# The score of each expert spread by a DMA from DRAM instead of a selection matmul, in a fused macaron block of two MoE layers on one core

## The reference, cut to what matters

```python
def _L0_ffn_ref(hidden_states, router_w, router_b, gate_up_proj, gate_up_bias, down_proj, down_bias):
    B, S, H, E, K, I = (1, 64, 128, 16, 4, 128)
    ALPHA, LIMIT = (1.702, 7.0)
    x = hidden_states.reshape(-1, h)
    logits = x @ router_w + router_b
    topv, topi = jax.lax.top_k(logits, K)
    topw = jax.nn.softmax(topv, axis=-1)
    one_hot = (topi[..., None] == jnp.arange(E)).astype(topw.dtype)
    scores = jnp.einsum('tk,tke->te', topw, one_hot)
    gu = jnp.einsum('th,ehf->tef', x, gate_up_proj) + gate_up_bias
    gate = jnp.minimum(gu[..., ::2], LIMIT)
    up = jnp.clip(gu[..., 1::2], -LIMIT, LIMIT)
    glu = gate * jax.nn.sigmoid(gate * ALPHA)
    act = (up + 1.0) * glu
    expert_out = jnp.einsum('tei,eih->teh', act, down_proj) + down_bias
    out = jnp.einsum('te,teh->th', scores, expert_out)

x = x + 0.5 * _L0_ffn_ref(_layernorm(x), ...)      # first FFN
x = x + _L0_attn_ref(_layernorm(x), ...)           # state-space mixer, with an inner layer norm
x = x + 0.5 * _L0_ffn_ref(_layernorm(x), ...)      # the same FFN and weights again
```

## Time and profile before

| | |
|---|---|
| Time, median of 3 runs | 824.15 us (819.81 to 825.55) |
| The profiled execution: time, span | 822.77 us, 821.0 us |
| Engine busy in it | PE 718.6, DVE 497.7, ACT 568.1, POOL 261.4 us |
| Jobs, first selection matmul to last | 28.3 to 394.4 us |
| The passes two to eight (jobs 16 to 127) | 80.7 to 396.6 us |

### The profile page before, as it was taken

One profiled execution on the slowest core, in us unless ns is written; L12 is line 12 of the kernel. 1 busy time (PEld: TensorE's weight loads), 2 busy tenths in 40 slices (PEclk: granted clock), 3 DMA queues, 4 the chain that ended last, 5 costly groups with the idle time before them and its releaser, 6 DMA issues.

```text
span 821.0 us, 11243 instructions
## 1 busy us (share of the span) xinstructions
PE 718.6 (88%) x3736; PEld 429.3 (52%) x3736; DVE 497.7 (61%) x1268; ACT 568.1 (69%) x800; POOL 261.4 (32%) x289
## 2 busy tenths in 40 slices
PE   2889889899898999999686696999999999999587
PEld 2567667676676777878564352323323232233364
DVE  4789878789788888888566442244423232222464
ACT  4557675667777666555344446999999999999243
POOL 2286466665666554555412000021200000000020
PEclk9999999999999999999758776999999999999958
DMA  9100000000000000000000269100079400000001
GB/s 269 42 0 2 0 1 1 0 1 2 0 1 1 0 1 2 0 1 1 0 1 0 52 127 196 36 1 1 1 134 194 85 2 1 1 1 1 3 1 51
DMA packets 14989, 24.94 MB, mean 30 GB/s; under 512 B 2720, under 2 KB 11376, under 8 KB 13424
## 3 DMA queue, kind: packets, MB, share of 16 engines
q1 hardware_dynamic: 13776, 23.79, 13.2%
q0 software_dynamic: 224, 0.34, 0.2%
q10 hardware_dynamic: 928, 0.06, 0.1%
HBM read 6.35 MB, written 1.05 MB: 9 GB/s over the span
## 4 chain that ended last, share of the span: by engine, by line
ACT 28%; PE 14%; issue 9%; DVE 5%; POOL 4%; ACTq 0%; POOLq 0%; DVEq 0%
ACT raw_w L782 25%; POOL act_parts L539 3%; PE bank L1341 2%; PE bank L1342 2%; PE bank L1343 2%; PE bank L1628 1%; ACT xt L609 1%; PE bank L1381 1%; PE bank L1535 1%; PE bank L1396 1%; PE bank L1612 1%; DVE xn_parts L875 1%; PE bank L1397 1%; POOL rstd L488 1%; DVE stats L865 1%
## 5 line engine op out<-in xcount | busy, mean ns | idle before, releaser
L782 ACT ACTIVATE raw_w<-bank,minus_c 128x1024 f32<-128x1024 f32 x256 | 259.3, 1161 | 4.8 <-DVE bank L1221 2.6
L539 POOL TENSOR_TENSOR act_parts<-act,act_parts 128x512 fp32r<-128x512 f32 x128 | 168.5, 1318 | 151.1 <-ACT act_parts L671 148.2
L657 ACT ACTIVATE glu<-bank,b_gate 128x512 f32<-128x512 f32 x128 | 88.1, 688 | 113.5 <-PE bank L1343 112.8
L1221 DVE TENSOR_TENSOR bank<-bank,fix 128x256 f32<-128x256 f32 x128 | 55.3, 433 | 180.4 <-PE bank L1612 180.4
L1341 PE MATMUL bank<-xn_parts,w_hi 128*128 128x512 f32 x256 | 108.0, 422 | 15.7 <-DVE up L999 8.0
L1343 PE MATMUL bank<-xn_parts,w_hi 128*128 128x512 f32 x256 | 103.0, 402 | 0.0
L1342 PE MATMUL bank<-xn_parts,w_lo 128*128 128x512 f32 x256 | 102.4, 400 | 0.0
L999 DVE TENSOR_SCALAR up<-bank,b_up 128x512 f32<-128x512 f32 x113 | 84.2, 745 | 24.7 <-PE bank L1343 24.0
L1003 DVE SCALAR_TENSOR_TENSOR bank<-glu,bank 128x512 f32<-128x512 f32 x128 | 87.9, 687 | 7.3 <-ACT glu L657 7.1
L1012 DVE SCALAR_TENSOR_TENSOR act<-up,bank 128x512 f32<-128x512 f32 x128 | 87.9, 687 | 4.4
L671 ACT ACTIVATE act_parts<-act 128x512 fp32r<-128x512 f32 x128 | 80.1, 626 | 14.8 <-DVE act L1012 14.5
(11 more groups left out here) (195 smaller groups left out, 1071.2 us busy)
## 6 DMA issues: line engine op xcount, KB each, us to landing
raw_w<-in_gate_up SPq DMA_DIRECT2D x4, 512.0 KB, 9.1
w_lo<-gelu_parts SPq DMA_DIRECT2D x8, 256.0 KB, 5.4
w_lo<-act_parts SPq DMA_DIRECT2D x8, 256.0 KB, 5.5
w_hi<-gelu_parts SPq DMA_DIRECT2D x6, 256.0 KB, 4.6
w_hi<-act_parts SPq DMA_DIRECT2D x6, 256.0 KB, 5.6
x_tok<-in_x SPq DMA_DIRECT2D x4, 256.0 KB, 4.4
raw_w<-in_down SPq DMA_DIRECT2D x4, 256.0 KB, 8.5
grow<-in_grow SPq DMA_DIRECT2D x1, 1024.0 KB, 7.4
```

The lines of the kernel that those rows point to most:

```text
L539: pool.tensor_tensor(act_lo[:, j % NACT, :], act[:, j % NACT, :], act_hi[:, j % NACT, :].bitcast(F32), ALU.subtract).then_inc(s["lo_ready" ...
L657: eng.activation(glu[:, j % 2, :], bank[:, G, :], ACT.Gelu_apprx_sigmoid, bias=b_gate[:, e:e + 1]).then_inc(s["glu_ready"], 1)
L782: eng.activation(probs[:, u % NP, :], pair, ACT.Exp, bias=minus_c[:, b:b + 1])\
L1221: eng.tensor_tensor(pair, pair, turned, ALU.mult)\
```

## The change

From job 16 on the selection matmul isn't issued. The scores of the seven chunks that follow the first one go to a DRAM tensor and come back spread:

- `router_scores` transposes 48 columns instead of 32: `share_hl` now also holds the unsplit score, so bank 7 has it on partitions 32 to 47.
- ACT's `router_out` has one more copy (L687 of the changed kernel, 16x512) of those rows into `score_f`, a corner of the `grow` tensor, ahead of the one into `score_t`.
- SP stores them (`store_scores`, one DMA of 32 KB per chunk) and, five jobs ahead of its use, reads one expert's row of 512 scores onto 128 partitions (`spread_score`, one DMA of 256 KB written per job). Five buffers take turns: three in `grow`, two in `early`, whose former contents (`raw_s`) are used up by then. A buffer is refilled when `glu_s_ready` says that DVE has read it.
- ACT's gelu output goes to PSUM bank S[j % 2], not to `glu` in SBUF. It waits for `act_ready` of job j - 2 instead of `glu_s_ready` of job j - 2.
- DVE multiplies bank S by the spread row in SBUF.
- `grow` is loaded after the last job instead of at the start.

```diff
+SPREAD_AHEAD = 5
+def spread_by_pe(j):
+    return j < E0
...
+        share_hl = sb("share_hl", [128, 2, TPC, 3 * E0])
+        share = share_hl[:, :, :, 2 * E0:3 * E0]
...
+        grow_parts = grow[:].rearrange("p i (h t) -> p (i h) t", t=CH)
+        spread = [grow_parts[:, 0, :], grow_parts[:, 1, :], grow_parts[:, 2, :], early[:, 0, 0:CH], early[:, 0, CH:L]]
+        score_f = grow_parts[2 * E0:3 * E0, 3, :]
+        scores_out = nc.dram_tensor("scores", (2, NC, E0, CH), F32, kind="Internal").ap()
...
+            def store_scores(r, c):
+                sp.wait_ge(s["score_f_ready"], r * NC + c)
+                sp.dma_start(scores_out[r, c], score_f).then_inc(s["scores_stored"], 16)
+
+            def spread_score(j):
+                e, c, f = j % E0, j // E0 % NC, j // E0 // NC
+                if e == 0:
+                    sp.wait_ge(s["scores_stored"], 16 * (f * NC + c))
+                if j == E0:
+                    sp.wait_ge(s["squares_ready"], 2)
+                if j >= E0 + len(spread):
+                    sp.wait_ge(s["glu_s_ready"], j - len(spread) + 1)
+                sp.dma_start(spread[j % len(spread)], scores_out[f, c, e][None, :].to_broadcast([128, CH]))\
+                  .then_inc(s[f"spread{j % len(spread)}"], 16)
+
+            for slot in range(FIRST_SLOT, JOBS):
+                for chain, r in (("in", 0), ("ssm", 1)):
+                    for c in range(NC):
+                        if BASE[chain][c] + STEPS["act"][chain]["out"] + 1 == slot and r * NC + c >= 1:
+                            store_scores(r, c)
+                if not spread_by_pe(slot + SPREAD_AHEAD) and slot + SPREAD_AHEAD < JOBS:
+                    spread_score(slot + SPREAD_AHEAD)
+
             sp.wait_ge(s["down_done"], JOBS)
+            sp.dma_start(grow[:], io["grow"]).then_inc(s["prep_loaded"], 16)
...
+                if r < 2 and kr >= 1:
+                    if kr >= 2:
+                        eng.wait_ge(s["scores_stored"], 16 * (kr - 1))
+                    eng.activation(score_f, bank[nr:nr + E0, scores_bank(r), :], ACT.Copy)\
+                       .then_inc(s["score_f_ready"], 1)
...
-                if j >= 2:
-                    eng.wait_ge(s["glu_s_ready"], j - 1)
-                eng.activation(glu[:, j % 2, :], bank[:, G, :], ACT.Gelu_apprx_sigmoid,
+                if spread_by_pe(j):
+                    if j >= 2:
+                        eng.wait_ge(s["glu_s_ready"], j - 1)
+                    out = glu[:, j % 2, :]
+                else:
+                    eng.wait_ge(s["act_ready"], j - 1)
+                    out = bank[:, S[j % 2], :]
+                eng.activation(out, bank[:, G, :], ACT.Gelu_apprx_sigmoid,
...
-                eng.wait_ge(s["s_ready"], j + 1)
-                eng.scalar_tensor_tensor(out=bank[:, S[j % 2], :], in0=glu[:, j % 2, :], scalar=GLU_AT_LIMIT,
-                                         in1=bank[:, S[j % 2], :], op0=ALU.min, op1=ALU.mult)\
+                if spread_by_pe(j):
+                    eng.wait_ge(s["s_ready"], j + 1)
+                    gated, weight = glu[:, j % 2, :], bank[:, S[j % 2], :]
+                else:
+                    eng.wait_ge(s[f"spread{j % len(spread)}"], 16 * ((j - E0) // len(spread) + 1))
+                    gated, weight = bank[:, S[j % 2], :], spread[j % len(spread)]
+                eng.scalar_tensor_tensor(out=bank[:, S[j % 2], :], in0=gated, scalar=GLU_AT_LIMIT,
+                                         in1=weight, op0=ALU.min, op1=ALU.mult)\
...
-                if j >= 2:
-                    pe.wait_ge(s["act_ready"], j - 1)
-                if e == 0:
-                    pe.wait_ge(s["score_ready"], nth(f, c))
-                pe.matmul(bank[:, S[j % 2], :], sel0_all[:, e, :], score_all[:, at], start=True, stop=True)\
-                  .then_inc(s["s_ready"], 1)
+                if spread_by_pe(j):
+                    if j >= 2:
+                        pe.wait_ge(s["act_ready"], j - 1)
+                    if e == 0:
+                        pe.wait_ge(s["score_ready"], nth(f, c))
+                    pe.matmul(bank[:, S[j % 2], :], sel0_all[:, e, :], score_all[:, at], start=True, stop=True)\
+                      .then_inc(s["s_ready"], 1)
```

13 lines of the change are left out of this document (6 added, 7 removed).

## The result

Over 19 runs the changed kernel took 816.83 us (813.07 to 823.05), the kernel before 821.53 in 19 runs between them (815.68 to 825.92). The ratio on record is 0.9956, 95% interval 0.9935 to 0.9977: 0.44% or 3.6 us faster. The medians lie 4.7 us apart, since the ratio is not taken from them. The forecast was 15.9 us. Ratios leave out two disturbed executions, one of e7 (the profiled one) and one of e11. The profiled execution took 818.78 us, 4.0 less than the one of before.

A forecast was written before the change was run, and what follows sets the result against it. PE was taken to bound the jobs for nine tenths of passes two to eight, DVE close behind. Terms -3.5 - 14.4 + 2.0 = -15.9 us gave 806.9 profiled, 808 median; forecast 802 to 813, range 798 to 822.

The forecast's parts named there:

- the sign: Whole kernel: faster, by 15.9 us; chance 0.77 of being faster by over 1%.
- the last pass: Last pass: DVE's 15 waits for PE each shorten by 0.23 us, 3.5 us gained; 2.07 us per job.
- the spreads under cover: Spreads by DMA: landing in 4.4 to 5.4 us, hidden within five jobs, 10.3 us; cost zero.
- its 689 ns unchanged: DVE's product: one input from a bank and one from SBUF as before, 687 ns; cost zero.
- `grow` late: Load of `grow` after the jobs: takes 7.4 us with 57 us of cover; cost zero.
- Rival (4): Product's wait for its spread row: spreads too slow, kernel slower, 1001 us if transfers did not overlap; chance 0.05.
- the term of 14.4 us for passes two to seven: Passes two to seven: 47 DVE waits shrink by two thirds of 0.46 us each, 14.4 us gained; ends 10.4 and 22.1.
- rivals (1): DVE takes the bound at once, PE's gain is waited away, only the last pass gains: 814 to 823 us; chance 0.16.
- Rival (3): PE, idle more, loses granted clock: four more slow stretches, 8 us, would leave 816 us; chance 0.07.
- ACT's additional copy: Seven copies of 0.57 us on ACT, between a high part and the next gelu: costs 2.0 us, from 0 to 4.0.
- The gelu into PSUM: ACT's gelu writing to a bank: 688 ns taken as unchanged, under 1 us either way.

The follow-up runs named there:

- e7: Changed kernel without stores and spreads, scores left out from the second pass on, ACT's additional copy kept; 0.9924 to the kernel before, median 817.9 us.
- e11: Changed kernel with one ACT copy, down projection three slots behind, and two banks each for gate and up; 0.9924 to the kernel before, 814.0 us.
- e18: Changed kernel with `UP_ON_ACT` empty, so no `up` half on ACT; 0.9831 to the kernel before, 806.6 us.
- e1: Changed kernel with a zero-weight matmul of the same size in place of each removed selection matmul; 1.0079 to the kernel before, 826.8 us.
- e17: Kernel before with `UP_ON_ACT` empty, so no `up` half on ACT; 0.9954 to the kernel before, 816.3 us.
- e8: Changed kernel with one ACT copy of 48 rows into `score_t` in place of two; 0.9915 to the kernel before, 813.9 us.
- e3: Kernel before with DVE's product on half the columns from the second pass on; 0.9976 to the kernel before, 817.8 us.
- e4: Changed kernel with DVE's product on half the columns from the second pass on; 0.9899 to the kernel before, 812.0 us.
- e6: Changed kernel with two banks each for gate and up, plus a zero-weight matmul for each removed one; 1.0024 to the kernel before, 823.3 us.
- e5: Changed kernel with two banks each for the gate and up matmuls from the second pass on; 0.9952 to the kernel before, 817.2 us.
- e12: e11 with a zero-weight matmul per job in place of the selection matmul; 0.9982 to the kernel before, 818.3 us.
- e13: Kernel before with the mixer's gelu and router's exponential replaced, removing ACT's table loads in the passes; 0.9847 to the kernel before, 811.0 us.
- e14: Changed kernel with the mixer's gelu and router's exponential replaced, removing ACT's table loads in the passes; 0.9776 to the kernel before, 805.1 us.
- e10: Changed kernel with one ACT copy and the down projection three slots behind instead of two; 0.9896 to the kernel before, 811.2 us.
- e2: Changed kernel without stores, spreads and additional copy, scores left out from the second pass on; 0.9918 to the kernel before, 812.8 us.
- e15: Changed kernel with one ACT copy and `UP_ON_ACT` empty; 0.9779 to the kernel before, 805.8 us.
- e16: Changed kernel with one ACT copy, down projection three slots behind and `UP_ON_ACT` empty; 0.9744 to the kernel before, 802.7 us.

## Why the prediction was right or wrong

**Right:** the sign, and the last pass (3.2 us for 3.5; 2.06 us per job for 2.07); the spreads under cover, landing in 3.2 us where 4.4 to 5.4 were allowed, with no wait of the product and its 689 ns unchanged; `grow` late at no cost. Rival (4) fell: 91 GB/s over the window, 115 in e18's seventh pass. The Trainium skill's 103 GB/s for streams at a pitch of 4 MiB (DMA: Bandwidth & Descriptors, Latency and other measured facts) did not carry over to reads of one and the same row.

**Wrong:** the term of 14.4 us for passes two to seven, "I keep two thirds: 47 waits x 0.46 x 2/3". 0.5 us came. The time of 816.8 us lies where the forecast had put rivals (1) and (3), not in its own 802 to 813. The step took each wait of DVE for PE as an independent piece that shrinks by what PE gains. But of the 16.2 us outside the last pass none went: 34 waits became 19, of the same total. They seem mostly passed on: PE late because ACT's burst, DVE's own side work or POOL's split had held it before. Where PE is held, what it gained since the last hold is lost whole, which is what the burst's 0.56 us shows in that one place. The forecast gave a third for 30 such stalls; PE's stalls weren't a fixed set that spares the rest: they grew by 15 us of the 25.8 (17 as counted ahead of the weight loads), and by 14 to 15 between e1 and the changed kernel and between e17 and e18. And 13 of the 47 waits were for ACT's `up`: 11.7 us became 11.9. I had them shrink like the others; they hung on ACT. The forecast had left 7.9 of the 25.8 us to stalls (25.8 less 3.5 and 14.4), and it was 15. And it had nothing for the granted clock, which added 7. These two, 7 us each, are the gap between 15.9 and what came, less the 2.0 that it had for the copy; the 7 of the clock is an account from one execution of each kernel (below).

**Also off:** ACT's additional copy, 3 to 4 us by e8 for "I take half, 2.0", by way of the clock rather than of ACT's busy time as far as the traces show. The gelu into PSUM is 27 ns shorter; the Trainium skill (PSUM, Specifications) was right on the sign, and at five waits of the product for it this is 0.1 us.

**Rival (3), the clock**, had 0.07 and came closest: it had four more stretches at the lower clock, 8 us and 816 in all. In the records of the granted clock the kernel before spends 10.2 us of passes two to eight at the lower level (0.98 over the window) and the changed one 27.3 (0.96). At the forecast's half of the time the additional 17 us are 8.5, by the starts of the matmuls 7. The profiled execution of the changed kernel is one with a low clock, 0.919 over the span for a mean of 0.925 of its runs, and 2 us above the median, so a usual one loses less. The run means show the same, mean clock over the whole span, matmul or kernel before on the left and without the matmul on the right:

| pair | clock | gain |
|---|---|---|
| before, after | 0.931, 0.925 | 0.44% |
| e3, e4 (light product) | 0.932, 0.924 | 0.77% |
| e6, e5 (two banks) | 0.933, 0.928 | 0.72% |
| e12, e11 (later down, two banks) | 0.929, 0.920 | 0.58% |
| e13, e14 (no table loads) | 0.937, 0.929 | 0.71% |
| e1, after | 0.928, 0.925 | 1.23% |
| e17, e18 (no `up` on ACT) | 0.935, 0.936 | 1.23% |

(0.931 is the mean over all series of the kernel before, whose means go from 0.930 to 0.933; each gain is good to some 0.2 to 0.6%.) In the two pairs where the clock changes by 0.003 or less the gain is 1.2%; where it falls by 0.005 to 0.009 it is 0.4 to 0.8%. The worst place is in the seventh pass. Windows of the changed kernel around it, and from its timeline the matmul behind a stop of PE, and DVE's wait 5 us later:

```profile
317.00:323.30 6.30, 4.08 (x18) 2.73 (x17) 6.13 (x22) 2.43 (x4) 2.58 (x2) 0.99 0.19 66
323.30:329.90 6.60, 6.53 (x15) 4.73 (x16) 3.64 (x9) 4.11 (x6) 2.41 (x2) 0.50 0.21 71
```

```profile
321.44 0.50 PE L1391 MATMUL bank<-xn_parts,w_hi 128*128 128x512 f32 x1 [1.32 <-DVE up L1044]
...
323.37 0.79 PE L1509 MATMUL bank<-score_t,db_hi 32*128 32x512 f32 x1 [0.97 <-DVE x L1069]
...
325.96 0.63 PE L1391 MATMUL bank<-xn_parts,w_hi 128*128 128x512 f32 x1
...
326.38 0.63 PE L1392 MATMUL bank<-xn_parts,w_lo 128*128 128x512 f32 x1
...
328.76 0.75 DVE L1044 TENSOR_SCALAR up<-bank,b_up 128x512 f32<-128x512 f32 x1 [2.86 <-PE bank L1393]
```

DVE is busy all through the first window (6.13 of 6.30) and PE stops 1.32 and 0.97 us for it; then the clock is 0.50 for 6.6 us, a matmul is 0.63 long instead of 0.40, and now DVE waits 2.86 for PE. The seventh pass of other kernels without the matmul, e8, e10 and e14, shows what hangs on that fall:

```profile
314.60:356.20 41.60, 39.05 (x155) 29.85 (x155) 35.52 (x72) 24.88 (x39) 20.64 (x16) 0.92 0.34 100
313.50:351.50 38.00, 35.71 (x157) 27.72 (x156) 35.07 (x71) 24.80 (x39) 20.66 (x16) 1.00 0.36 109
305.80:344.40 38.60, 35.90 (x154) 27.68 (x155) 35.44 (x71) 22.72 (x38) 20.72 (x16) 1.00 0.34 108
```

With the fall it takes 41.0 to 41.7 us (after, e2, e8, e11), without it 37.1 to 38.6 (e10, e14, e15, e16, e18), with half as long a fall 39.7 and 40.3 (e4, e5); the kernel before takes 40.8, without a fall. These kernels differ in more than the clock, but in this pass the gain is there wherever the clock stays. PE stands more often with the matmul gone, and the clock fell behind such stands. The Trainium skill (TensorE: Matmul & The Clock Gate, Part 1) ties the gate to activity, and these rows agree. But no run held the clock and changed the rest, so that the clock took up to 7 us is read from rows that go together, not shown by an experiment.

**Open:** why PE stands 14 us and more longer in every pair, whatever is taken away. Passes two to five take 46 to 52 us in all these kernels but e13 and e14 (44 to 47). DVE's load (e4), banks (e5), room (e10) and table loads (e14) each moved the change's worth by 4 us or less. Why the list should move the clock is open too. Of e1's 6.5 us the copy is 3 to 4 and the kept matmul's place at most 1.6; 1 to 2 us have no name.

## What to carry to other kernels

Taking work off the engine that is busiest paid in full only where that engine runs from job to job without being stopped: here in the last pass, and there at once up to the next engine's pace. Elsewhere count the places at which it is held by a burst of another engine; in the one looked at here, what it had gained since the last one was gone. A wait "for PE" right behind a burst may be the burst's, not PE's. And put a price on the clock in the sum: what was taken off PE here made it stand more, and with that 17 us of the window went to the lower clock.

When the balance of two engines has changed, try again the lists that were set for the old one (here `UP_ON_ACT`, worth 10 us, where the change itself gave some 4), and rather than put a new instruction, however short, on a helper engine at its crowded place, fold it into one that is there (e8, 3 to 4 us).

## What the runs showed of the hardware

- Reading one 2 KB row of DRAM onto 128 partitions (256 KB) lands in 3.0 to 4.6 us, median 3.2, faster than the 4.4 us of 256 KB of different rows, four of them queued at the start; 112 of them beside the jobs cost no engine anything that e8 against e2 could show.
- ACT's gelu on 128x512 f32 took 661 ns with its output in a bank and 688 in SBUF, the plain copy of 16 rows 591 and of 32 rows 570.
- With 112 matmuls less, PE was granted less clock: 0.96 in the window instead of 0.98, and run means 0.003 to 0.009 lower in six pairs. In the seventh, without `up` on ACT, it wasn't: 0.98 for 0.99 in the window, run means 0.936 for 0.935.
- At the lower clock a 512-column matmul followed the one before it after 0.43 us instead of 0.23 (325.96 and 326.38 in the changed kernel's timeline).
